# A decoder layer on one core: the last output projection of the second stage issued at twice the density, with new orders on four engines behind it

## The chip, the core and the metric

The kernel runs on one NeuronCore of a Trainium2 chip. The metric is the time of one execution on the device, in microseconds, taken as the median of several runs. The engines that matter here are TensorE (PE in the rows, with PEld for its weight loads), VectorE (DVE), ScalarE (ACT), GpSimd (POOL) and SyncE (SP), which only issues DMAs. Each engine works through its own queue strictly in the order in which the program wrote it; engines wait for one another by semaphores.

## The reference

The input is 32 sequences ("tiles", 0 to 31) of 128 rows by 1024 columns, and a context of the same size. For each tile:

```python
x = _layernorm(x + _L0_attn_ref(x, wq, wk, wv, wo))      # causal attention, 32 heads, 8 kv heads
x = _layernorm(x + _L0_xattn_ref(x, ctx, weight))        # 3-tap convolution, inputs scaled by cosine similarities
x = _layernorm(x + _L0_ffn_ref(x, A, B, Wr, br))         # 8 rank-16 adapters weighted by a softmax router
# in _L0_xattn_ref:
out = jnp.einsum('bit,oi->bot', inp_unf * att, w_flat)   # inp_unf: 3 shifted copies, att: similarities, repeated
# in _L0_ffn_ref:
low = jnp.einsum('bsd,hrd->bshr', x, A)                  # rank reduction, 1024 -> 128 (and 8 router logits)
out = jnp.einsum('bshr,hor,bsh->bso', low, B, scores)    # gates, then expansion 128 -> 1024
```

Everything is float32. Large products are made of three TensorE passes: both operands are split into a high part and the rest (`hi`, `lo`), and high x high, high x rest and rest x high are added in PSUM.

## The kernel before

The program has two stages in one launch. The first makes the attention of every tile and stores it. The second, `part2`, takes each tile through the output projection, the first norm, the convolution, the second norm, the adapters and the third norm. The change lies in the end of the second stage alone.

**The second stage is a software pipeline over tiles.** In step t the engines work on four tiles at once, by the names in the code `o = t` (projection), `c = t-1` (first norm and convolution), `f = t-2` (second norm, rank reduction, router) and `z = t-3` (expansion, third norm). `steps` runs `step(t, ...)` for the last tiles unrolled; what is left of the last tiles after step 31 is written out by hand behind it. Which instruction comes next on an engine is decided by that text and by nothing else.

What each function issues:

- PE: `project(t, par, n, k)` issues 3 passes, 48 in all for a tile, 24 into each half `wo_ps0`, `wo_ps1`. `convolve(t, m)`, m = 0 to 5, issues 3 passes and needs product m; m = 0 to 2 is the first half of the columns, 3 to 5 the second. `turn_x2` makes 4 transposes of the second norm's result, `reduce_rank` contracts these to 136 columns (`low_done`), `turn_low` transposes the gated result, `expand` issues 6 passes.
- DVE: `add(t, par, n, half)` adds the residual to the result of stage n (0 projection, 1 convolution, 2 adapters), `count` takes its statistics and `average` mean and variance. `multiply(t, par, m)` makes product m (similarities times shifted rows). `route`, `gate_low` and `low_lt` serve the adapters.
- ACT: `normalise1`, `normalise2`, `normalise3` apply the three norms, `high_prod(t, m)` makes the high part of product m, `copy_x2` fetches the transposes from PSUM, `gates` the exponentials, `high_lt` the high part of the turned gated result.
- POOL: `invert_root(t, n)` makes the scale of norm n and its shift (the pair at lines 1482 and 1484), `low_prod(t, m)` the rest of product m. One product therefore passes DVE, ACT, POOL and PE, in this order, and three buffers (`PB = 3`) are in flight.

**The last step before.** In step 31 PE has 16 slots, one projection triple in each, and between them, by the table `CONV_AT`, what belongs to tiles 28, 29 and 30: convolutions of tile 29 (products 4, 5), of tile 30 (0 to 3), the expansion of tile 28, the transposes and rank reduction of tile 29. Then, by hand, come products 4 and 5 of tile 30, the expansion of tile 29, the convolution of tile 31 with the transposes of tile 30 behind its second product, and the adapters of tiles 30 and 31. The accumulators of the adapters of tile 30 are `wo_ps`, since the projection no longer needs them; the others use `ffn_ps`. Line numbers of the profile in this part: L1134 projection, L1145 convolution, L1160 transposes, L1167 rank reduction, L1173 `turn_low`, L1179 expansion, L1237, L1242 and L1247 the three additions, L1254 statistics, L1271 products, L1382 high parts, L1387, L1393 and L1416 the three norms, L1399 `copy_x2`, L1405 gates, L1410 `high_lt`, L1488 the rest of a product.

Of the kernel before, what the change touches and what calls it, by code (L numbers as in the profile page):

```python
# [22 lines left out]
B, S, D = 32, 128, 1024  # L23
P = 128
KT = D // P
# [33 lines left out]
def after(t, per, k):  # L59

    return t * per + k
# [917 lines left out]
def part2(nc, ctx, weights, raw, halves, wo_ps, handoff, x, wa, br, ident, ot_dram, sim_dram, out):  # L979
# [12 lines left out]
    PB = 3  # L992
# [64 lines left out]
    LEAD, TAIL = 6, 5  # L1057
    UNITS = 2 * TAPS
# [67 lines left out]
    def _(pe):  # L1126
# [36 lines left out]
        def reduce_rank(t):  # L1163

            wait(pe, xt_in, after(t, 2, 2))
            for k in range(KT):
                mm = pe.matmul(ffn_place(t)[0][:, 0:LOWW], xt[:, k], wa_t[:, k * LOWW:(k + 1) * LOWW],  # L1167
                               start=(k == 0), stop=(k == KT - 1))
            mm.then_inc(low_done, 1)

        def turn_low(t):
            wait(pe, gated_done, after(t, 1, 1))
            pe.transpose(ffn_place(t)[1][:, 0:S], gated[:], id_t[:]).then_inc(low_turned, 1)  # L1173
# [26 lines left out]
                if valid(o) and not at_step(o, 0) and not (at_step(o, 1) and s < KT):  # L1200
                    project(o, par, s // KT, s % KT)

        steps(pe, step, 0, B - 1, LEAD, TAIL - 3)

        convolve(B - 2, 4)
        turn_low(B - 3)
        convolve(B - 2, 5)
        expand(B - 3)
        for m in range(UNITS):
            convolve(B - 1, m)  # L1210
            if m == 1:
                turn_x2(B - 2, 0, 0)
                turn_x2(B - 2, 0, 1)
        reduce_rank(B - 2)
        turn_x2(B - 1, 1, 0)
        turn_low(B - 2)
        turn_x2(B - 1, 1, 1)
        expand(B - 2)
        reduce_rank(B - 1)
# [4 lines left out]
    def _(dve):  # L1224
# [25 lines left out]
        def count(t, n, half):  # L1250

            src = y3 if n == 2 else yz[n]
            dve.wait_ge(added[n], after(t, 2, half + 1))
            dve.bn_stats(stats[n][:, half], src[:, half * BANK:(half + 1) * BANK]).then_inc(counted[n], 1)  # L1254
# [79 lines left out]
            if valid(f):  # L1334
                gate_low(f)

        steps(dve, step, 0, B - 1, LEAD, TAIL - 3)

        def finish(t):

            for half in range(2):
                add(t, t % 2, 2, half)
                count(t, 2, half)
            average(t, 2)

        add(B - 1, 1, 0, 1)
        count(B - 1, 0, 1)
        average(B - 1, 0)
        low_lt(B - 3)
        add(B - 2, 0, 1, 1)  # L1350
        count(B - 2, 1, 1)
        average(B - 2, 1)
        for m in range(PB):
            multiply(B - 1, 1, m)
        finish(B - 3)
        for m in range(PB, UNITS):
            multiply(B - 1, 1, m)
        add(B - 1, 1, 1, 0)
        count(B - 1, 1, 0)
        add(B - 1, 1, 1, 1)  # L1360
        count(B - 1, 1, 1)
        average(B - 1, 1)
        route(B - 2)
        gate_low(B - 2)
        low_lt(B - 2)
        finish(B - 2)
# [6 lines left out]
    def _(act):  # L1373
# [73 lines left out]
            if valid(c):  # L1447
                high_prod(c, 5)

        steps(act, step, 0, B - 1, LEAD, TAIL - 3)  # L1450

        high_lt(B - 3)
        normalise1(B - 1, 1)
        normalise2(B - 2, 0)
        for m in range(UNITS):
            high_prod(B - 1, m)
            if m in (2, 3):
                copy_x2(B - 2, m - 2)
        normalise3(B - 3, 1)
        normalise2(B - 1, 1)  # L1460
        gates(B - 2)
        copy_x2(B - 1, 0)
        high_lt(B - 2)
        copy_x2(B - 1, 1)
        gates(B - 1)
        high_lt(B - 1)
# [3 lines left out]
    @block.gpsimd  # L1470
    def _(pool):
        def low_o(t, par, half):
            cols = slice(half * D // 2, (half + 1) * D // 2)
            wait(pool, o_hi, after(t, 1, 1))
            hi, lo = (os_t[:, par, part].rearrange("p t s -> p (t s)")[:, cols] for part in range(2))
            pool.tensor_tensor(lo, oraw[:, par, cols], hi.bitcast(F32), ALU.subtract).then_inc(o_lo, 1)  # L1476

        def invert_root(t, n):

            wait(pool, var_done[n], after(t, 1, 1))  # L1480
            wait(pool, normed[n], after(t - 1, 1, 1))
            pool.tensor_tensor(rstd[n][:], var[n][:], power[:], ALU.pow).then_inc(rstd_done[n], 1)  # L1482
            pool.wait_ge(rstd_done[n], after(t, 1, 1))
            pool.tensor_tensor(shift[n][:], nmean[n][:], rstd[n][:], ALU.mult).then_inc(shifted[n], 1)

        def low_prod(t, m):
            wait(pool, prod_hi, after(t, UNITS, m + 1))
            pool.tensor_tensor(prods[:, m % PB, 1], prod[:, m % PB], prods[:, m % PB, 0].bitcast(F32),  # L1488
                               ALU.subtract).then_inc(prod_lo, 1)

        pool.wait_ge(set_up, 3)

        def step(t, par):
            c, f, z = t - 1, t - 2, t - 3
            early = not at_step(t, 0) and not at_step(t, 1)
            if valid(c):
                invert_root(c, 0)
            if at_step(t, 1):
                low_o(2, 0, 0)
                low_o(2, 0, 1)  # L1500
            if valid(t + 1) and early:
                low_o(t + 1, 1 - par, 0)
            if valid(c):
                low_prod(c, 0)
            if valid(f):
                invert_root(f, 1)
            if valid(c):
                low_prod(c, 1)
            if valid(z):
                invert_root(z, 2)  # L1510
            if valid(c):
                low_prod(c, 2)
            if valid(t + 1) and early:
                low_o(t + 1, 1 - par, 1)
            if valid(c):
                for m in range(3, UNITS):
                    low_prod(c, m)

        steps(pool, step, 0, B - 1, LEAD, TAIL - 3)

        invert_root(B - 1, 0)
        invert_root(B - 2, 1)
        for m in range(UNITS):
            low_prod(B - 1, m)
            if m == 2:
                invert_root(B - 3, 2)
        invert_root(B - 1, 1)
        invert_root(B - 2, 2)
        invert_root(B - 1, 2)
# [48 lines left out]
```

## Time and profile before

| | us |
|---|---|
| median of three runs | 1408.07 |
| lowest and highest of them | 1407.62, 1410.24 |
| span of the profiled execution, first to last instruction | 1404.9 |
| what the median has beyond that span (1408.07 - 1404.9) | 3.2 |
| busy in the span: PE, DVE, POOL, ACT | 1359.3, 1094.9, 984.3, 931.8 |
| last projection triple of tile 31 ends, in the span | 1363.7 |
| last norm of tile 31 ends (1400.54 + 1.24) | 1401.8 |

Of the profiled execution only the span is given; what lies around its first and last instruction is taken as the 3.2 us of the table. A step of the second stage lasts 19.5 us (in the chain of waits the first four transposes of a tile come at 1336.51 and of the next at 1356.03). The clock that is granted to TensorE is 1.00 of full speed in nearly all of the span; its dips lie in the last 40 us.

### The profile page before, as it was taken

Reading aid. Unit: us, or ns where it says so; the run is one execution under the profiler, and the core shown is the slowest. Engines: PE = TensorE matmul, PEld = TensorE weight load, DVE = VectorE, ACT = ScalarE, POOL = GpSimd, SP = SyncE. Lnnn points to the kernel's source line nnn. Section 1 sums busy time; section 2 is a strip of 40 time slices with the busy share of each in tenths; the row PEclk is TensorE's granted clock in tenths of the full one; section 3 lists DMA queues with packets and bytes.
Section 4 is the critical chain, followed back from the end, with each engine's and each line's share of the span. In section 5 each row is a group of like instructions: output and inputs, shape, how many; then the busy total and the mean of one; then the engine's idle time right before and its main releaser. Section 6 shows DMA issues by size and latency. Waiting matters only on the chain.

```text
span 1404.9 us, 32306 instructions
## 1 busy us (share of the span) xinstructions
PE 1359.3 (97%) x8294; PEld 1058.0 (75%) x8294; DVE 1094.9 (78%) x3869; ACT 931.8 (66%) x3258; POOL 984.3 (70%) x936
## 2 busy tenths in 40 slices
PE   8999999999999999999986999999999999999995
PEld 6777777777777777777754788888888888888873
DVE  5887887878788787787775678887788877888774
ACT  5888888878788887888884455554555545555443
POOL 4777776777777677777774667766777667776653
PEclk9999999999999999999998999999999999999997
DMA  7354545445453544545478865657656666676751
GB/s 264 96 152 123 159 116 158 128 136 159 114 159 117 155 137 129 159 115 164 124 208 242 181 162 157 166 153 171 157 157 165 156 171 156 160 161 158 157 120 45
DMA packets 108861, 213.03 MB, mean 152 GB/s; under 512 B 26640, under 2 KB 32272, under 8 KB 108816
## 3 DMA queue, kind: packets, MB, share of 16 engines
q1 hardware_dynamic: 108480, 211.73, 56.5%
q10 hardware_dynamic: 336, 0.79, 0.2%
q8 instruction: 18, 0.29, 0.1%
q14 instruction: 27, 0.22, 0.1%
HBM read 131.83 MB, written 34.47 MB: 118 GB/s over the span
## 4 chain that ended last, share of the span: by engine, by line
PE 87%; POOL 3%; DMA 2%; SPq 2%; DVE 2%; issue 2%; ACT 2%; ACTq 0%; DVEq 0%; POOLq 0%
PE wo_ps L479 34%; PE wo_ps L1134 23%; PE conv_ps L1145 9%; PE s_ps L509 5%; PE pv_ps L522 4%; PE ffn_ps L1167 4%; PE ffn_ps L1179 3%; PE ffn_ps L1160 2%; PE turn_ps L498 2%; SPq L320 1%; POOL prods L1488 1%; ACT pexp L767 1%; DMA pt<-in_wqkv 1%; DMA raw<-in_xT 1%; PE turn_ps L488 0%
## 5 line engine op out<-in xcount | busy, mean ns | idle before, releaser
L479 PE MATMUL wo_ps<-weights,halves 128*128 128x512 f32 x2304 | 570.7, 400 | 3.5 <-DVE weights L681 3.5
L479 PEld LDWEIGHTS wo_ps<-weights,halves 128*128 128x128 f32 x2304 | 422.8, 189 | 137.8 <-issue 53.8
L767 ACT ACTIVATE pexp<-sm,smin 128x128 f32<-128x128 f32 x1024 | 398.0, 391 | 99.0 <-DVE smin L618 98.0
L1134 PE MATMUL wo_ps<-weights,halves 128*128 128x512 f32 x1464 | 393.2, 401 | 1.0 <-PEq L143 1.0
L1488 POOL TENSOR_TENSOR prods<-prod,prods 128x512 fp32r<-128x512 f32 x192 | 259.3, 1359 | 131.0 <-ACT prods L1382 126.0
L906 POOL TENSOR_TENSOR pn<-pexp,prec 128x512 f32<-128x512 f32 x256 | 265.4, 1041 | 98.1 <-DVE prec L625 98.1
L1134 PEld LDWEIGHTS wo_ps<-weights,halves 128*128 128x128 f32 x1464 | 267.1, 189 | 58.1 <-issue 1.8
L618 DVE CUSTOM_DVE_ANT_0 sm<-s_ps,mask_t 128x128 f32<-128x128 f32 x1024 | 231.9, 282 | 24.9 <-PE s_ps L509 19.6
L1382 ACT CAST prods<-prod 128x512 fp32r<-128x512 f32 x192 | 118.9, 621 | 165.5 <-DVE prod L1271 127.9
L1271 DVE TENSOR_TENSOR prod<-att,x 128x512 f32<-128x512 f32 x192 | 186.6, 987 | 13.3 <-DMA att<-sim_scratch 8.4
L767 ACT ACTIVATION_READ_ACCUMULATOR pexp<-sm,smin 128x1 f32 x1024 | 193.4, 189 | 0.0
L633 DVE STREAM_TRANSPOSE blocks<-pn 128x512 f32<-128x512 f32 x256 | 178.0, 695 | 6.6 <-POOL pn L906 6.3
L1145 PE MATMUL conv_ps<-prods,weights 128*128 128x512 f32 x576 | 169.4, 403 | 12.6 <-POOL prods L1488 12.6
L1145 PEld LDWEIGHTS conv_ps<-prods,weights 128*128 128x128 f32 x576 | 109.1, 191 | 40.9 <-POOL prods L1488 16.7
L901 POOL TENSOR_TENSOR xn<-rot,y 128x512 f32<-128x512 f32 x64 | 83.7, 1308 | 70.9 <-DVE y L605 70.8
L1254 DVE BATCH_NORM_STATS2 stats<-y 128x6 f32<-128x512 f32 x190 | 128.8, 691 | 4.5
L1482 POOL TENSOR_TENSOR moments<-moments,power 128x1 f32<-128x1 f32 x96 | 76.6, 798 | 64.2 <-DVE moments L1262 62.8
L880 POOL TENSOR_TENSOR halves<-raw,halves 128x512 fp32r<-128x512 f32 x62 | 80.7, 1302 | 27.1 <-ACT halves L740 27.1
L625 DVE RECIPROCAL prec<-psum_row 128x4 f32<-128x4 f32 x256 | 44.9, 175 | 69.8 <-ACT pexp L767 69.8
L600 DVE TENSOR_TENSOR rot<-wo_ps,rope_t 128x512 f32<-128x512 f32 (+1 forms) x96 | 56.7, 591 | 45.9 <-PE wo_ps L479 44.1
L1476 POOL TENSOR_TENSOR halves<-raw,halves 128x512 fp32r<-128x512 f32 x60 | 90.8, 1515 | 0.0
L618 DVE DVE_READ_ACCUMULATOR2_ANT smin<- 128x1 f32 x1024 | 85.0, 83 | 0.0
(103 smaller groups left out, 1636.5 us busy)
## 6 DMA issues: line engine op xcount, KB each, us to landing
att<-sim_scratch SPq DMA_DIRECT2D x192, 252.0 KB
pt<-blocks SPq DMA_DIRECT2D x636, 64.0 KB, 2.0
ctx_t<-in_ctx SPq DMA_DIRECT2D x32, 576.0 KB, 5.2
raw<-in_xT SPq DMA_DIRECT2D x32, 512.0 KB, 3.9
xn<-in_x SPq DMA_DIRECT2D x32, 512.0 KB, 7.6
out<-late SPq DMA_DIRECT2D x32, 512.0 KB, 6.2
ot_scratch<-ot SPq DMA_DIRECT2D x63, 256.0 KB, 2.1
raw<-ot_scratch SPq DMA_DIRECT2D x31, 512.0 KB, 6.8
```

Of the source, the lines that this page charges most:

```text
L479: mm = pe.matmul(qkv_ps[(par + g) % 2][:], xs[:, par, xl, k], w_sb[:, wl, g, k], start=(k == 0 and n == 0), stop=(k == KT - 1 and n == 2))
L618: ins = dve.tensor_tensor_reduce(sm[:, c % 2, i * P:(i + 1) * P], s_ps[i][:, j * P:(j + 1) * P], mask_t[:], 1.0, 3e38, ALU.add, ALU.min, s ...
L633: dve.transpose(blocks[:, u, :, j], pn[:, c % 2].rearrange("p (i b k) -> p b i k", i=NI, b=QB)).then_inc(turned, 1)
L767: ins = nc.scalar.activation(pexp[:, c % 2, i * P:(i + 1) * P], sm[:, c % 2, i * P:(i + 1) * P], ACT.Exp, bias=smin[:, c % 2, i:i + 1], sc ...
L906: pool.tensor_tensor(pn[:, c % 2].rearrange("p (i s) -> p i s", i=NI), pexp[:, c % 2].rearrange("p (i s) -> p i s", i=NI), prec[:, c % 2]. ...
L1134: mm = pe.matmul(wo_ps[n][:], os_t[:, par, ol, k], wo_sb[:, wl, k, n * BANK:(n + 1) * BANK], start=(k == 0 and m == 0), stop=(k == KT - 1 ...
L1145: mm = pe.matmul(conv_ps[h][:], wx_sb[:, wl, k], prods[:, m % PB, xl], start=(k == 0 and n == 0), stop=(k == TAPS - 1 and n == 2))
L1254: dve.bn_stats(stats[n][:, half], src[:, half * BANK:(half + 1) * BANK]).then_inc(counted[n], 1)
L1271: dve.tensor_tensor(prod[:, m % PB], att[:, k, h * BANK:(h + 1) * BANK], x1[:, par, h * BANK + k:h * BANK + k + BANK], ALU.mult).then_inc( ...
L1382: nc.scalar.copy(prods[:, m % PB, 0], prod[:, m % PB]).then_inc(prod_hi, 1)
L1476: pool.tensor_tensor(lo, oraw[:, par, cols], hi.bitcast(F32), ALU.subtract).then_inc(o_lo, 1)
L1488: pool.tensor_tensor(prods[:, m % PB, 1], prod[:, m % PB], prods[:, m % PB, 0].bitcast(F32), ALU.subtract).then_inc(prod_lo, 1)
```

## The change

The loop of steps now ends with step 30, and step 31 is written out by hand. On PE it has eight slots with two projection triples each, so that the 48 passes of tile 31 come with less of other work between them: the transposes, rank reduction and expansion of tile 29 and products 3 to 5 of tile 30 are moved behind the projection. In the convolution of tile 31 the transposes of tile 30 stand ahead of product 4, no longer ahead of product 2, and its rank reduction ahead of product 5. DVE, ACT and POOL get new orders to go with it. No arithmetic is added or taken away.

```diff
-        steps(pe, step, 0, B - 1, LEAD, TAIL - 3)
+        steps(pe, step, 0, B - 2, LEAD, TAIL - 4)
+        for s in range(KT):
+            if s == 1:
+                convolve(B - 3, 4)
+                turn_low(B - 4)
+            if s == 3:
+                expand(B - 4)
+            if s == 4:
+                convolve(B - 3, 5)
+            if s > 4:
+                convolve(B - 2, s - 5)
+            for k in (2 * s, 2 * s + 1):
+                project(B - 1, 1, k // KT, k % KT)
+        turn_x2(B - 3, 1, 0)
+        turn_x2(B - 3, 1, 1)
+        convolve(B - 2, 3)
+        reduce_rank(B - 3)
         convolve(B - 2, 4)
+        convolve(B - 2, 5)
         turn_low(B - 3)
-        convolve(B - 2, 5)
         expand(B - 3)
         for m in range(UNITS):
-            convolve(B - 1, m)
-            if m == 1:
+            if m == 4:
                 turn_x2(B - 2, 0, 0)
                 turn_x2(B - 2, 0, 1)
-        reduce_rank(B - 2)
+            if m == 5:
+                reduce_rank(B - 2)
+            convolve(B - 1, m)
+        turn_low(B - 2)
         turn_x2(B - 1, 1, 0)
-        turn_low(B - 2)
         turn_x2(B - 1, 1, 1)
...
# DVE, of the order written out for step 31 and behind it
+        add_and_count(B - 1, 0, 1)
         average(B - 1, 0)
+        multiply(B - 2, 0, 5)
+        add_and_count(B - 2, 1, 0)
+        route(B - 3)
+        multiply(B - 1, 1, 0)
+        gate_low(B - 3)
+        multiply(B - 1, 1, 1)
         low_lt(B - 3)
+        multiply(B - 1, 1, 2)
+        add_and_count(B - 2, 1, 1)
         average(B - 2, 1)
+        add(B - 3, 1, 2, 0)
+        add(B - 3, 1, 2, 1)
+        multiply(B - 1, 1, 3)
...
# ACT
+        high_prod(B - 1, 1)
+        high_prod(B - 1, 2)
         normalise2(B - 2, 0)
+        high_prod(B - 1, 3)
+        copy_x2(B - 2, 0)
+        high_prod(B - 1, 4)
+        copy_x2(B - 2, 1)
+        high_prod(B - 1, 5)
...
# POOL
+        low_prod(B - 1, 0)
+        low_prod(B - 1, 1)
         invert_root(B - 2, 1)
-        for m in range(UNITS):
+        for m in range(2, UNITS):
             low_prod(B - 1, m)
-            if m == 2:
-                invert_root(B - 3, 2)
+        invert_root(B - 3, 2)
```

PE at the start of step 31. In the kernel before, from the last triple of tile 30 and the first of tile 31 on:

```order
 L1134 MATMUL wo_ps<-weights,halves 128x512 x3
-L1134 MATMUL wo_ps<-weights,halves 128x512 x6
-L1145 MATMUL conv_ps<-prods,weights 128x512 x3
-L1173 MATMUL ffn_ps<-id_t,gated 128x128
-L1134 MATMUL wo_ps<-weights,halves 128x512 x6
-L1179 MATMUL ffn_ps<-weights,lt 128x512 x6
-L1134 MATMUL wo_ps<-weights,halves 128x512 x3
-L1145 MATMUL conv_ps<-prods,weights 128x512 x3
-L1134 MATMUL wo_ps<-weights,halves 128x512 x15
+L1134 MATMUL wo_ps<-weights,halves 128x512 x9
+L1145 MATMUL conv_ps<-prods,weights 128x512 x3
+L1173 MATMUL ffn_ps<-id_t,gated 128x128
+L1134 MATMUL wo_ps<-weights,halves 128x512 x12
+L1179 MATMUL ffn_ps<-weights,lt 128x512 x6
+L1134 MATMUL wo_ps<-weights,halves 128x512 x6
+L1145 MATMUL conv_ps<-prods,weights 128x512 x3
```

Ahead of the expansion of tile 28 (L1179) stood three triples of tile 31 (the first x6 row holds one of tile 30), and now six; ahead of the convolution that ends tile 29 (the second L1145) stood four, and now eight.

PE in the convolution of tile 31, before (the accumulators' numbers are shown; `wo_ps` holds the transposes and the rank reduction of tile 30):

```order
L1145 MATMUL conv_ps0<-prods,weights 128x512 x6
L1160 MATMUL wo_ps0<-id2_t,late 128x128 x4
L1160 MATMUL wo_ps1<-id2_t,late 128x128 x4
L1145 MATMUL conv_ps0<-prods,weights 128x512 x3
L1145 MATMUL conv_ps1<-prods,weights 128x512 x9
L1167 MATMUL wo_ps0<-wa_t,xt 128x136 x8
```

And now:

```order
L1145 MATMUL conv_ps0<-prods,weights 128x512 x9
L1145 MATMUL conv_ps1<-prods,weights 128x512 x3
L1160 MATMUL wo_ps0<-id2_t,late 128x128 x4
L1160 MATMUL wo_ps1<-id2_t,late 128x128 x4
L1145 MATMUL conv_ps1<-prods,weights 128x512 x3
L1167 MATMUL wo_ps0<-wa_t,xt 128x136 x8
L1145 MATMUL conv_ps1<-prods,weights 128x512 x3
```

The transposes have moved from behind the second product to behind the fourth, and the rank reduction from behind the last product to ahead of it.

DVE from the first norm of tile 31 to product 3 of tile 31, before:

```order
L1262 TENSOR_SCALAR moments<-mv0 128x1
L1294 TENSOR_TENSOR lt<-ffn_ps1,lt 128x128
L1242 TENSOR_TENSOR y1<-conv_ps1,x1 128x512
L1254 BN_STATS stats1<-y1 128x6
L1259 BN_AGGR mv1<-stats1 128x2
L1261 TENSOR_SCALAR moments<-mv1 128x1
L1262 TENSOR_SCALAR moments<-mv1 128x1
L1271 TENSOR_TENSOR prod<-att,x1 128x512 x3
```

And now (line numbers are those of the changed text, L1288 a product, L1259 the addition of the convolution):

```order
L1288 TENSOR_TENSOR prod<-att,x1 128x512
L1302 RECIPROCAL grec<-gsum 128x1
L1304 SCALAR_TENSOR_TENSOR gated<-ffn_ps0,grec,gate 128x128
L1288 TENSOR_TENSOR prod<-att,x1 128x512
L1311 TENSOR_TENSOR lt<-ffn_ps1,lt 128x128
L1288 TENSOR_TENSOR prod<-att,x1 128x512
L1259 TENSOR_TENSOR y1<-conv_ps1,x1 128x512
L1271 BN_STATS stats1<-y1 128x6
L1276 BN_AGGR mv1<-stats1 128x2
L1278 TENSOR_SCALAR moments<-mv1 128x1
```

The second half of tile 30's convolution is now added behind the first three products of tile 31, where it was added ahead of them, and between those products stand the gating and `low_lt` of tile 29.

## Rows read from the trace of the kernel before

**Rows 1.** Stretches: length; busy (instructions) of each engine; PEclk; DMA share; GB/s.
```profile
1320.00:1340.00 20.00, 20.00 (x100) 16.61 (x99) 16.24 (x34) 10.30 (x16) 14.62 (x15) 1.00 0.65 137
...
1372.00:1376.80 4.80, 4.80 (x15) 3.95 (x16) 3.87 (x7) 1.03 (x3) 3.52 (x4) 0.50 0.02 5
1376.80:1383.50 6.70, 5.32 (x28) 3.67 (x26) 2.94 (x5) 2.74 (x5) 3.76 (x3) 1.00 0.20 78
1383.50:1387.00 3.50, 0.87 (x6) 0.55 (x6) 1.00 (x7) 1.81 (x4) 0.74 (x2) 1.00 0.00 0
1387.00:1390.40 3.40, 3.40 (x11) 2.69 (x12) 1.08 (x3) 1.09 (x3) 0.00 (x0) 0.51 0.00 0
```

**Rows 2.** Timeline of PE: start, length, instruction, count, [idle before <-released by].
```profile
1346.86 1.56 PE L1179 MATMUL ffn_ps<-weights,lt 128*128 128x512 f32 x6
...
1348.95 0.86 PE L1145 MATMUL conv_ps<-prods,weights 128*128 128x512 f32 x3
1349.65 3.60 PE L1134 MATMUL wo_ps<-weights,halves 128*128 128x512 f32 x15
...
1362.79 0.86 PE L1134 MATMUL wo_ps<-weights,halves 128*128 128x512 f32 x3
...
1371.95 2.93 PE L1145 MATMUL conv_ps<-prods,weights 128*128 128x512 f32 x6 [4.32 <-POOL prods L1488]
1374.68 1.91 PE L1160 MATMUL wo_ps<-id_t,late 128*128 128x128 f32 x8
...
1378.29 0.96 PE L1145 MATMUL conv_ps<-prods,weights 128*128 128x512 f32 x3 [0.82 <-POOL prods L1488]
...
1380.77 0.96 PE L1145 MATMUL conv_ps<-prods,weights 128*128 128x512 f32 x3 [0.27 <-POOL prods L1488]
1381.57 2.01 PE L1167 MATMUL wo_ps<-wa_t,xt 128*128 128x136 f32 x16
1386.01 0.66 PE L1160 MATMUL ffn_ps<-id_t,late 128*128 128x128 f32 x4 [2.43 <-ACT late L1393]
...
1387.89 2.84 PE L1179 MATMUL wo_ps<-weights,lt 128*128 128x512 f32 x6
```

**Rows 3.** Timeline of DVE.
```profile
1349.86 0.69 DVE L1242 TENSOR_TENSOR y<-conv_ps,x 128x512 f32<-128x512 f32 x1
...
1363.69 0.69 DVE L1237 TENSOR_TENSOR y<-wo_ps,xn 128x512 f32<-128x512 f32 x1 [0.66 <-PE wo_ps L1134]
...
1368.03 1.89 DVE L1271 TENSOR_TENSOR prod<-att,x 128x512 f32<-128x512 f32 x3 [0.18 <-ACT x L1387]
...
1373.26 2.88 DVE L1271 TENSOR_TENSOR prod<-att,x 128x512 f32<-128x512 f32 x3
...
1381.77 0.69 DVE L1242 TENSOR_TENSOR y<-conv_ps,x 128x512 f32<-128x512 f32 x1 [2.85 <-PE conv_ps L1145]
...
1389.58 0.69 DVE L1247 SCALAR_TENSOR_TENSOR y<-wo_ps,late 128x512 f32<-128x512 f32 x1 [1.74 <-PE wo_ps L1179]
```

**Rows 4.** Timeline of POOL.
```profile
1351.95 0.93 POOL L1482 TENSOR_TENSOR moments<-moments,power 128x1 f32<-128x1 f32 x1 [0.17 <-DVE moments L1262]
...
1353.20 1.30 POOL L1488 TENSOR_TENSOR prods<-prod,prods 128x512 fp32r<-128x512 f32 x1
...
1370.63 3.74 POOL L1488 TENSOR_TENSOR prods<-prod,prods 128x512 fp32r<-128x512 f32 x3 [1.86 <-ACT prods L1382]
```

**Rows 5.** Timeline of ACT.
```profile
1366.65 1.24 ACT L1387 ACTIVATE x<-y,moments 128x1024 f32<-128x1024 f32 x1 [1.89 <-POOL moments L1484]
...
1375.77 0.59 ACT L1399 COPY xt<-wo_ps 128x512 f32<-128x512 f32 x1 [4.18 <-PE wo_ps L1160]
1376.26 0.62 ACT L1382 CAST prods<-prod 128x512 fp32r<-128x512 f32 x1
...
1384.72 1.24 ACT L1393 ACTIVATE late<-y,moments 128x1024 f32<-128x1024 f32 x1 [5.18 <-POOL moments L1484]
...
1400.54 1.24 ACT L1416 ACTIVATE late<-y,moments 128x1024 f32<-128x1024 f32 x1 [4.51 <-POOL moments L1484]
```

More of the change, by code:

```diff
@@ L1335, in step, with add_and_count @@
                 gate_low(f)
-        steps(dve, step, 0, B - 1, LEAD, TAIL - 3)
+        steps(dve, step, 0, B - 2, LEAD, TAIL - 4)
+        def add_and_count(t, n, half):
+            add(t, t % 2, n, half)
+            count(t, n, half)
         def finish(t):
             for half in range(2):
-                add(t, t % 2, 2, half)
-                count(t, 2, half)
+                add_and_count(t, 2, half)
             average(t, 2)
-        add(B - 1, 1, 0, 1)
-        count(B - 1, 0, 1)
-        average(B - 1, 0)
+        add_and_count(B - 2, 0, 1)
+        average(B - 2, 0)
+        low_lt(B - 4)
+        add(B - 4, 0, 2, 0)
+        add(B - 4, 0, 2, 1)
+        multiply(B - 2, 0, 0)
+        add_and_count(B - 3, 1, 1)
+        average(B - 3, 1)
+        multiply(B - 2, 0, 1)
+        count(B - 4, 2, 0)
+        count(B - 4, 2, 1)
+        average(B - 4, 2)
+        multiply(B - 2, 0, 2)
+        add_and_count(B - 1, 0, 0)
+        multiply(B - 2, 0, 3)
+        multiply(B - 2, 0, 4)
+        add_and_count(B - 1, 0, 1)
+        average(B - 1, 0)
+        multiply(B - 2, 0, 5)
[4 more added lines that the diff above has]
+        multiply(B - 1, 1, 1)
         low_lt(B - 3)
-        add(B - 2, 0, 1, 1)
-        count(B - 2, 1, 1)
+        multiply(B - 1, 1, 2)
+        add_and_count(B - 2, 1, 1)
         average(B - 2, 1)
[L1353 to L1361, printed above, removed]
+        add(B - 3, 1, 2, 0)
+        add(B - 3, 1, 2, 1)
+        multiply(B - 1, 1, 3)
+        count(B - 3, 2, 0)
+        multiply(B - 1, 1, 4)
+        count(B - 3, 2, 1)
+        average(B - 3, 2)
+        multiply(B - 1, 1, 5)
+        add_and_count(B - 1, 1, 0)
+        route(B - 2)
+        add_and_count(B - 1, 1, 1)
         average(B - 1, 1)
-        route(B - 2)
         gate_low(B - 2)
@@ L1448, in step @@
                 high_prod(c, 5)
-        steps(act, step, 0, B - 1, LEAD, TAIL - 3)
+        steps(act, step, 0, B - 2, LEAD, TAIL - 4)
+        high_lt(B - 4)
+        normalise1(B - 2, 0)
+        high_prod(B - 2, 0)
+        high_prod(B - 2, 1)
+        normalise2(B - 3, 1)
+        high_prod(B - 2, 2)
+        normalise3(B - 4, 0)
+        high_prod(B - 2, 3)
+        high_prod(B - 2, 4)
+        copy_x2(B - 3, 0)
+        copy_x2(B - 3, 1)
+        high_prod(B - 2, 5)
+        normalise1(B - 1, 1)
+        gates(B - 3)
+        high_prod(B - 1, 0)
         high_lt(B - 3)
-        normalise1(B - 1, 1)
+        high_prod(B - 1, 1)
+        high_prod(B - 1, 2)
         normalise2(B - 2, 0)
-        for m in range(UNITS):
-            high_prod(B - 1, m)
-            if m in (2, 3):
-                copy_x2(B - 2, m - 2)
+        high_prod(B - 1, 3)
[3 more added lines that the diff above has]
+        high_prod(B - 1, 5)
         normalise3(B - 3, 1)
+        gates(B - 2)
         normalise2(B - 1, 1)
-        gates(B - 2)
+        high_lt(B - 2)
         copy_x2(B - 1, 0)
-        high_lt(B - 2)
         copy_x2(B - 1, 1)
@@ L1517, in step @@
                     low_prod(c, m)
-        steps(pool, step, 0, B - 1, LEAD, TAIL - 3)
+        steps(pool, step, 0, B - 2, LEAD, TAIL - 4)
+        invert_root(B - 2, 0)
+        low_prod(B - 2, 0)
+        invert_root(B - 3, 1)
+        low_prod(B - 2, 1)
+        invert_root(B - 4, 2)
+        for m in range(2, 5):
+            low_prod(B - 2, m)
         invert_root(B - 1, 0)
+        low_prod(B - 2, 5)
+        low_prod(B - 1, 0)
+        low_prod(B - 1, 1)
         invert_root(B - 2, 1)
-        for m in range(UNITS):
+        for m in range(2, UNITS):
             low_prod(B - 1, m)
-            if m == 2:
-                invert_root(B - 3, 2)
+        invert_root(B - 3, 2)
         invert_root(B - 1, 1)
```

## Prediction

> **What bounds the kernel now.** I read the stretches first. In the middle of the second stage TensorE is busy for all of the 20 us from 1320 to 1340, at full clock, and every other engine has room [rows 1]. Up to the last projection, then, only what PE has to do decides. Behind it the picture turns: the timeline of PE shows idle 4.32, 0.82 and 0.27 us for `low_prod`, then 2.43 us for the second norm [rows 2], and the chain goes from one engine to the next. So a change that only shuffles PE's work can gain up to the last projection, by putting it first, and from there on the orders of DVE, ACT and POOL count as much. I then followed the last 60 us engine by engine [rows 2 to 5], and worked the new order with the same durations and the same gaps between engines. All times below are in the scale of the old trace, "was" is its value.
>
> **The clock.** PEclk was 0.50 from 1372 to 1376.8, after the idle 4.32 us, and 0.51 from 1387 to 1390.4, after 2.43 us [rows 1, 2]: that is 1.2 in place of 2.4 GHz. The trace gives prices: two convolutions 2.93 us, eight transposes 1.91, an expansion 2.84, against 0.86 for one convolution, 0.66 for four transposes and 1.56 for an expansion at full clock [rows 2].
>
> **Step 1, the head of step 31.** 15 passes take 3.60 us with 0.16 of emptying at the end, so a triple has 0.69 [rows 2]; I use 0.70, for a convolution too, 0.11 for `turn_low` and 1.40 for an expansion. Step 31 starts three triples, a convolution and `turn_low` ahead of 1346.86, at 1343.96. Now six triples stand ahead of the expansion of tile 28: it comes at 1348.97, 2.1 late. Eight stand ahead of the convolution that ends tile 29: 1343.96 + 9 x 0.70 + 0.11 + 1.40 = 1351.8, was 1348.95, 2.8 late. DVE adds it at 1352.7, was 1349.86 [rows 3]; behind that addition, in the unchanged order of DVE, wait the norm of tile 29 and products 1 to 4 of tile 30, all 2.8 late. What hid the old wait of these products was slack against PE's position; that cover is now gone.
>
> **Step 2, the projection.** Without waits it would end after 16 triples, 5 convolutions, `turn_low` and an expansion, 1343.96 + 21 x 0.70 + 1.51 + 0.16 = 1360.3; was 1362.79 + 0.86 = 1363.65 [rows 2]: 3.3 earlier. But POOL makes the root of tile 29 at 1351.95 and the rest of product 1 at 1353.20 for 1.30 [rows 4], now 2.8 later: ready at 1357.3. PE stands ready for it at 1351.8 + 6 x 0.70 = 1356.0 and waits 1.3. Product 2 is ready about 2.6 after product 1 (its low part of 1.30 and the root of another norm at some 1.25 lie behind the low part of product 1, as that lies 1.25 behind the root at 1351.95): PE, ready at 1359.4, waits 0.5. The projection ends at 1362.2, a lead of 1.5, and not of 3.3. The two loads of similarities for tile 31 are issued 2.8 later as well, their cover is the time to product 0 of tile 31 (some 9 us); they cost nothing.
>
> **Step 3, the first norm of tile 31.** DVE adds at 1362.2 (was 1363.69). Between the mean and the norm there now stands product 5 of tile 30 on DVE (0.68) and its high part on ACT (0.62), ahead of `normalise1` in ACT's queue: 1362.2 + 1.95 (addition and statistics at 0.69 each, the mean, and what lies between them) + 0.68 + 0.04 + 0.62 = 1365.5. `normalise1` was at 1366.65 [rows 5]: a lead of 1.1.
>
> **Step 4, where the lead goes.** Before, DVE added the second half of tile 30 while it waited for this norm. Now it does so behind three products of tile 31, `gate_low` and `low_lt`. Three products in a row took 1.89 us, but 2.88 where POOL was making low parts at the same time (1373.26, POOL at work from 1370.63 to 1374.37) [rows 3, 4]; an operation held like that ends about 0.55 after POOL's. So product 0 starts at 1366.9, product 2 at 1368.9 and ends, held by POOL, at 1370.2. The addition ends at 1370.8, statistics and mean take 1.4 more, and POOL needs 0.9 for root and shift [rows 4]; the low part of product 2 stands behind them, 1373.1 to 1374.4. Its old place was the last third of 1370.63 to 1374.37 [rows 4]. The lead is nil. Product 3, held until 1374.9, is where it was.
>
> **Step 5, the last three products.** High part 1375.0 to 1375.6, low part (0.35 held) to 1377.3, convolution 3 at 1377.35, was 1378.29 [rows 2]: there ACT stood at `copy_x2` until 1375.77, waiting for the transposes, with the high part of product 3 behind it [rows 5]. Now both come later. Transposes at full clock to 1378.65, `copy_x2` 1378.7, only then the high part of product 4, 1379.2 to 1379.8, its low part to 1381.1, and convolution 4 at 1381.2. Product 5 is ready at 1382.4, but ahead of it stands the rank reduction, from 1381.9, which holds PE 1.85 (16 passes of 0.115; 2.01 with emptying [rows 2]): convolution 5 at 1383.7. It was at 1380.77. **DVE adds it at 1384.6, was 1381.77 [rows 3]: 2.85 late.** In the old order the transposes lay in time in which PE waited for POOL, and the rank reduction behind the last convolution, beside the addition and the mean. This is the term on which the forecast stands.
>
> **Step 6, the tail.** `normalise2` of tile 31 comes at 1384.72 + 2.85 = 1387.6 [rows 5], and ends at 1388.8. Now the gating of tile 30 is done ahead of it, so the expansion can follow the transposes directly: 1389.7, first half at DVE 1390.6, at full clock. It was at 1389.58 [rows 3], with the expansion at half clock. From that addition on nothing changes, and it was 12.2 to the end of the last norm at 1401.78 [rows 3, 5]. Sum at full clock throughout: +1.05.
>
> Now the clock. By the steps above PE is idle about 2.3 us before convolution 2 of tile 31 (from 1372.1), 2.2 before convolution 3, 2.2 before convolution 4 and 2.6 behind convolution 5, with only 0.86 of work between the first two. The stretch with 0.87 us of work in 3.50 was followed by half clock [rows 1]. So I count half clock twice: at convolution 3 and the transposes of tile 30 (2.93 / 2 - 0.86 = 0.6, and 1.91 / 2 - 0.66, 0.3 to 0.4, on the chain), 1.0; and at the transposes of tile 31 and the first half of the expansion of tile 30 (1.91 - 1.3 = 0.6 and 2.84 / 2 - 0.78 = 0.65, with the first pass after idle longer), 1.3 to 1.6. Together 1.05 + 1.0 + 1.5 = **+3.55**. The span becomes 1404.9 + 3.55 = 1408.45; with the 3.17 that the median has beyond the span, and so 1408.07 + 3.55 = **1411.6**. The order's own cost in this is bounded from below by the +1.05 and from above by a rank reduction at half clock, for which no row exists: between nothing and a doubling, 1.85 more. I take nothing, since the reduction follows 2 to 3 us of work, as the one at 1381.57 did; the range keeps it.
>
> The Trainium skill, "TensorE: Matmul & The Clock Gate", section "Why this matters for your kernels", asks for no idle gap of more than about 3 us between bursts of matmuls, or the clock drops. By it none of the new gaps would cost anything, and the sum would be +1.05. The trace disagrees: 2.43 us of idle time, with little work before, were followed by 0.51 [rows 1, 2]. I give it the second rival.
>
> **Rivals.** (A change below 0.2%, 2.8 us, can't be told from none in a measurement of this kernel.)
>
> *Faster.* The lead of 1.1 at the first norm of tile 31 lives on to the last convolution. For it: PE was idle 4.32 us there, and now has tile 29 to do in it, so that the clock may stay at 1.00, which was worth 0.6 on each convolution. It decides at POOL: if the low part of product 2 comes at 1371.5 and not behind the root of tile 30, product 3 follows at once, and the last convolution ends at 1380.6. With the tail at full clock (-1.4): 1408.07 - 1.1 - 1.4 = 1405.5. Against it: the order on POOL is strict, and the rank reduction still stands ahead of the last convolution.
>
> *The clock stays at full.* +1.05 alone: 1409.1. For it: gaps of 2.2 to 2.6 us are much shorter than 4.32. Against it: 2.43 was enough once.
>
> *Rank reduction at half clock as well,* and with it a third piece of the tail: 3.55 + 1.85 = +5.4, 1413.5.
>
> *The projection doesn't come earlier.* If DVE's products are held longer than in the old rows, PE waits for each of products 0 to 2 of tile 30 and the last triple ends where it did. Everything behind follows 1.1 later at most, since `normalise1` then has no lead: 1412.7. For it: POOL and DVE meet more often in the new order; against it: the five waits of step 2 are known from rows, and 1.8 us of the 3.3 are already counted as lost.
>
> **How the numbers follow.** The forecast, with half clock once or twice, +2.3 to +4.6: 0.52. Full clock: 0.18. Rank reduction at half clock: 0.11. No earlier projection: 0.09. Faster: 0.10. Slower than 1410.9 (1408.07 + 2.8) are nine tenths of the forecast's share less the cases at one dip, 0.43, and the two late cases, 0.20: 0.63. Faster than 1405.3: a little less than the faster case, 0.07, as its 1405.5 lies on the bound. The rest, 0.30, is no difference. The range reaches from 1407.5, which takes in full clock and leaves out the faster case, to 1414.5, beyond the case of 1413.5.
>
> **What would show it.** Right: last projection triple ends near 1362; `normalise1` of tile 31 near 1365.5; the low part of product 2 of tile 31 still at 1373, behind a root; PE idle before convolutions 2, 3 and 4 of tile 31 about 2 us each; the last convolution at 1383 to 1385, directly behind the rank reduction; PEclk 0.5 in a part of 1376 to 1391. Wrong: the last addition of the convolution before 1382, or a rank reduction that ends before its product is ready.

## The result, and the profile after

| | before | changed |
|---|---|---|
| median, us | 1409.57 | 1413.80 |
| lowest and highest | 1407.62, 1410.24 | 1409.80, 1414.49 |
| ratio, with its 95% interval | | 1.0029 [1.0018, 1.0041] |
| span of the profiled execution | 1404.9 | 1412.0 |
| start of step 31 to the end of the last norm | 57.8 | 62.8 |

The changed kernel is slower by 0.29% +- 0.11, some 4.1 us; 3.55 were forecast (the medians are over six runs each, three of them the ones shown before). The spans differ by 7.1, but 2.15 of this lie ahead of the change: the first triple of tile 31 starts at 1346.12 in the one execution and at 1343.97 in the other, though the program is the same up to there (over the profiles of this study that start lies between 1343.97 and 1347.83). So the two tails are compared from that triple on. For this result and the ten runs below, the timed difference to the kernel before and the difference of the tails differ by 1.4 us at most, by 0.1 on the mean: nothing points to a loss ahead of the tail. In the last line of the table and below, "at 18.2" is 18.2 us behind it.

PE after, from the last triple of tile 30 on (timeline: start, length, instruction, count, idle before it and its releaser); the rows answer to those of PE before [rows 2]:

```profile
1345.42 2.24 PE L1134 MATMUL wo_ps<-weights,halves 128*128 128x512 f32 x9
...
1353.82 0.87 PE L1145 MATMUL conv_ps<-prods,weights 128*128 128x512 f32 x3
...
1359.40 0.96 PE L1145 MATMUL conv_ps<-prods,weights 128*128 128x512 f32 x3 [1.01 <-POOL prods L1547]
1360.20 1.56 PE L1134 MATMUL wo_ps<-weights,halves 128*128 128x512 f32 x6
1361.97 0.97 PE L1145 MATMUL conv_ps<-prods,weights 128*128 128x512 f32 x3 [0.22 <-POOL prods L1547]
1362.78 1.55 PE L1134 MATMUL wo_ps<-weights,halves 128*128 128x512 f32 x6
...
1376.63 0.97 PE L1145 MATMUL conv_ps<-prods,weights 128*128 128x512 f32 x3 [1.93 <-POOL prods L1547]
1379.50 1.65 PE L1145 MATMUL conv_ps<-prods,weights 128*128 128x512 f32 x3 [1.90 <-POOL prods L1547]
1380.95 1.91 PE L1160 MATMUL wo_ps<-id_t,late 128*128 128x128 f32 x8
1384.54 1.65 PE L1145 MATMUL conv_ps<-prods,weights 128*128 128x512 f32 x3 [1.68 <-POOL prods L1547]
1385.98 3.04 PE L1167 MATMUL wo_ps<-wa_t,xt 128*128 128x136 f32 x16
1388.77 0.95 PE L1145 MATMUL conv_ps<-prods,weights 128*128 128x512 f32 x3
```

The x9 row holds one triple of tile 30, so step 31 starts at 1345.42 + 0.70. The reader is to see three things. The convolution that ends tile 29 comes at 1353.82, 7.7 behind the start, where it came at 5.0. PE waits 1.01 and 0.22 us for products of tile 30, and the last triple ends at 1364.33, at 18.2, where it ended at 19.7. And of the last three convolutions each has its own obstacle: the wait for product 3, then the transposes and a new wait, then the whole rank reduction, which runs ahead of the last one. That last one ends at 43.6; it ended at 37.8.

DVE, ACT and POOL after, the rows that answer to [rows 3 to 5]:

```profile
1372.45 0.68 DVE L1259 TENSOR_TENSOR y<-conv_ps,x 128x512 f32<-128x512 f32 x1
...
1375.57 1.56 DVE L1288 TENSOR_TENSOR prod<-att,x 128x512 f32<-128x512 f32 x1
...
1389.76 0.69 DVE L1259 TENSOR_TENSOR y<-conv_ps,x 128x512 f32<-128x512 f32 x1 [0.34 <-PE conv_ps L1145]
```

```profile
1374.54 0.55 POOL L1541 TENSOR_TENSOR moments<-moments,power 128x1 f32<-128x1 f32 x1 [0.85 <-DVE moments L1279]
1375.16 0.19 POOL L1543 TENSOR_TENSOR moments<-moments 128x1 f32<-128x1 f32 x1
1375.31 1.27 POOL L1547 TENSOR_TENSOR prods<-prod,prods 128x512 fp32r<-128x512 f32 x1
```

```profile
1367.71 1.24 ACT L1429 ACTIVATE x<-y,moments 128x1024 f32<-128x1024 f32 x1
...
1382.04 0.58 ACT L1441 COPY xt<-wo_ps 128x512 f32<-128x512 f32 x1 [4.26 <-PE wo_ps L1160]
1382.52 0.62 ACT L1424 CAST prods<-prod 128x512 fp32r<-128x512 f32 x1
...
1392.71 1.24 ACT L1435 ACTIVATE late<-y,moments 128x1024 f32<-128x1024 f32 x1 [2.86 <-POOL moments L1543]
```

The first norm of tile 31 starts at 21.6 (22.7 before), but POOL makes the low part of its product 2 only behind the root of tile 30, at 29.2 (29.1 before). The high part of product 4 stands behind `copy_x2`, which waits 4.26 us for the transposes. The second norm of tile 31 starts at 46.6; it started at 40.8.

The clock after (stretches: length; busy and instructions of PE, PEld, DVE, ACT, POOL; PEclk; DMA; GB/s), to be set beside [rows 1]:

```profile
1378.00:1388.00 10.00, 6.82 (x23) 5.73 (x24) 3.24 (x8) 3.35 (x5) 4.64 (x5) 0.50 0.00 1
1388.00:1394.80 6.80, 2.86 (x19) 2.19 (x19) 2.85 (x10) 1.89 (x5) 0.74 (x2) 0.99 0.19 77
1394.80:1398.30 3.50, 3.50 (x13) 2.92 (x12) 1.78 (x3) 0.98 (x2) 0.00 (x0) 0.51 0.00 0
```

Ten microseconds in a row at half clock, over the transposes and most of the rank reduction that now stand on the chain, and over two convolutions.

### The profile page after: what moved, and what is told of

Its sections match the earlier page's. It is cut to its first block, busy times and chain, and to the rows that moved or that the text cites. A ratio compares the mean times of both kernels' runs of the same rounds, so it can differ in the third digit from the quotient of the medians.

```text
span 1412.0 us, 32306 instructions
## 1 busy us (share of the span) xinstructions
PE 1362.4 (96%) x8294; PEld 1058.7 (75%) x8294; DVE 1094.0 (77%) x3869; ACT 932.3 (66%) x3258; POOL 984.2 (70%) x936
## 4 chain that ended last, share of the span: by engine, by line
PE 80%; DMA 5%; SPq 5%; DVE 3%; issue 3%; POOL 2%; ACT 2%; ACTq 0%; DVEq 0%; POOLq 0%
PE wo_ps L479 29%; PE wo_ps L1134 23%; PE conv_ps L1145 9%; PE s_ps L509 4%; PE ffn_ps L1167 4%; PE pv_ps L522 4%; SPq L320 3%; PE ffn_ps L1179 3%; DMA raw<-in_xT 2%; PE ffn_ps L1160 2%; PE turn_ps L498 1%; DMA att<-sim_scratch 1%; ACT pexp L767 1%; DMA pt<-in_wqkv 1%; DVE sm L618 1%
## 5 line engine op out<-in xcount | busy, mean ns | idle before, releaser
L1288 DVE TENSOR_TENSOR prod<-att,x 128x512 f32<-128x512 f32 x192 | 187.4, 990 | 14.0 <-DMA att<-sim_scratch 11.2
L1145 PE MATMUL conv_ps<-prods,weights 128*128 128x512 f32 x576 | 169.3, 402 | 12.8 <-POOL prods L1547 12.7
L1145 PEld LDWEIGHTS conv_ps<-prods,weights 128*128 128x128 f32 x576 | 108.2, 190 | 41.9 <-POOL prods L1547 17.9
L625 DVE RECIPROCAL prec<-psum_row 128x4 f32<-128x4 f32 x256 | 44.9, 175 | 75.8 <-ACT pexp L767 75.8
L509 PEld LDWEIGHTS s_ps<-kt,qt 32*128 32x128 f32 x2048 | 64.0, 188 | 29.2 <-issue 23.9
```

Of the source, the lines that this page charges most:

```text
L509: mm = pe.matmul(s_ps[i][:, j * P:(j + 1) * P], qt[rows, u, j * P:(j + 1) * P], kt[rows, par, u * P:(u + 1) * P], start=True, stop=True, t ...
L1288: dve.tensor_tensor(prod[:, m % PB], att[:, k, h * BANK:(h + 1) * BANK], x1[:, par, h * BANK + k:h * BANK + k + BANK], ALU.mult).then_inc( ...
```

## The experiments

All ratios are to the kernel before, run beside them on the same chip. The tail is the time from the first triple of tile 31 to the end of the last norm in the one profiled execution; it was 57.8 before and 62.8 changed. A second profile of the changed kernel, `changed_again` below, has 61.7; the kernel before has only one.

**The last two products: the rank reduction alone.**

```diff
-            if m == 5:
-                reduce_rank(B - 2)
             convolve(B - 1, m)
+        reduce_rank(B - 2)
```

with `route(B - 2)` behind `average(B - 1, 1)` on DVE.

> The changed kernel with the rank reduction of tile 30 behind the last convolution of tile 31, not ahead of it, and its router behind the mean of tile 31 on DVE. If the order of PE at the last two products is what costs (my theory), the last convolution no longer waits for 16 passes: about 2.1 us less than the changed kernel, so 1.0014 of the kernel before. If the time is lost in the head of step 31 and in the second norm of tile 30 (the first rival), the last product is late anyway and nothing moves: 1.0029. If only TensorE's clock costs (the second rival), nothing moves either, or up to 1 us for the reduction that the changed kernel ran at half clock.

Measured 1.0025 [1.0015, 1.0036], tail 61.0. The last convolution started at 39.6, not at 42.7, and the second norm of tile 31 at 44.8, not at 46.6. But the reduction moved to where it ran at half clock:

```profile
1386.23 0.97 PE L1145 MATMUL conv_ps<-prods,weights 128*128 128x512 f32 x3 [1.68 <-POOL prods L1546]
1387.47 1.21 PE L1145 MATMUL conv_ps<-prods,weights 128*128 128x512 f32 x3 [0.27 <-POOL prods L1546]
1388.47 3.46 PE L1167 MATMUL wo_ps<-wa_t,xt 128*128 128x136 f32 x16
```

A miss in time: the 1.0014 expected lies just outside, and the gain on the changed kernel is 0.0004, with about 0.0010 to either side of both ratios. Against `changed_again`, where the reduction ran at full clock, the last convolution starts 1.4 earlier (39.6, 41.0), so the reduction did stand in its way, but the second norm of tile 31 comes no earlier (44.8, 44.9). The rows of POOL and ACT say why:

```profile
1391.44 0.20 POOL L1542 TENSOR_TENSOR moments<-moments 128x1 f32<-128x1 f32 x1
```

```profile
1392.37 0.30 ACT L1446 ACTIVATE gate<-logit,nmax 128x8 f32<-128x8 f32 x1 [2.90 <-DVE nmax L1297]
...
1392.67 1.22 ACT L1434 ACTIVATE late<-y,moments 128x1024 f32<-128x1024 f32 x1
```

The scale of the norm is ready at 1391.64, but `gates` of tile 30 stands ahead of the norm in ACT's queue (in the kernel before it stood behind it), and waits for the late and slow reduction: 1.0 us. The edit took the reduction off PE's way to the last convolution and left it on the chain through ACT.

**The last two products: the transposes alone.**

```diff
-            if m == 4:
+            if m == 3:
                 turn_x2(B - 2, 0, 0)
                 turn_x2(B - 2, 0, 1)
```

> The changed kernel with the transposes of tile 30 one product earlier, ahead of the convolution of product 3 and not of product 4; nothing else. My theory: PE waits 1.9 us for product 3 there, the second norm of tile 30 is ready, so the transposes cost nothing, ACT gets its copies before the high part of product 4 and is no longer held: about 3.7 us less than the changed kernel, 1.0003 of the kernel before. First rival (head and second norm): no change, 1.0029. Clock rival: a little less, since PE's idle time is cut in two: 1.0022.

Measured 0.9998 [0.9989, 1.0007], tail 58.9. In the timed runs this one number moved takes back the loss, as expected, and both rivals as priced (1.0029 and 1.0022) fall; in the profiles the tail is 3.9 shorter than in the first execution of the changed kernel and 2.8 shorter than in the second, and still 1.1 longer than before. The rows of PE:

```profile
1374.50 1.28 PE L1145 MATMUL conv_ps<-prods,weights 128*128 128x512 f32 x3 [1.93 <-POOL prods L1547]
1375.58 1.91 PE L1160 MATMUL wo_ps<-id_t,late 128*128 128x128 f32 x8
1377.37 1.40 PE L1145 MATMUL conv_ps<-prods,weights 128*128 128x512 f32 x3
1379.55 0.96 PE L1145 MATMUL conv_ps<-prods,weights 128*128 128x512 f32 x3 [0.78 <-POOL prods L1547]
1380.35 2.02 PE L1167 MATMUL wo_ps<-wa_t,xt 128*128 128x136 f32 x16
1382.12 0.95 PE L1145 MATMUL conv_ps<-prods,weights 128*128 128x512 f32 x3
```

Product 3's convolution is no later (33.4 in both), product 4's comes at 35.6 and not at 38.4, and the wait ahead of it is 0.78 and not 1.68. The last convolution starts at 38.1. In `changed_again` it starts at 41.0, with the transposes at half clock and the rank reduction at full clock as here, so these 2.8 us are the order's above all.

**The clock.** Extra passes into an unused bank, where PE waits, in the changed kernel and in the one before:

```diff
+                pe.matmul(spare[:], wx_sb[:, 0, 0], wb_sb[:, 0, 0:BANK], start=True, stop=True)
...
+            fill((0, 0, 6, 6, 5, 0)[m])
             convolve(B - 1, m)
+        fill(8)
         turn_low(B - 2)
...
```

> The changed kernel with extra passes on PE into an unused PSUM bank where it waits in the tail: 6, 6 and 5 of 512 columns ahead of the convolutions of products 2, 3 and 4 of tile 31, 8 ahead of turn_low of tile 30, 4 each ahead of the transposes of tile 31 and turn_low of tile 31. They keep the clock at full speed and should end before what PE waits for. My sum at full clock: the order alone costs 1.05 us against the kernel before as it is, so 1.0007. If the clock costs nothing on the chain: 1.0029. If the clock is all of the loss: 1.0000 or below.

> The kernel before with such passes where PE waits: 14 ahead of the convolution of product 0 of tile 31, 8 ahead of the transposes of tile 31, 4 ahead of its turn_low. If the half clock from 1372 to 1376.8 and from 1387 to 1390.4 lies on the chain as I took it, about 1.9 us go: 0.9987 of the kernel before. If half clock only makes PE's waits shorter: 1.0000.

Measured 1.0019 [1.0009, 1.0029], tail 59.2, and 0.9993 [0.9985, 1.0002], tail 56.7. The timed runs leave this open: the first interval leaves out 1.0007 by little and reaches to 1.0029, the second holds 0.9987 and 1.0000 alike. The traces say more. In the changed kernel the clock is then full through the stretches in which it had dipped:

```profile
1377.00:1388.00 11.00, 9.52 (x53) 7.56 (x51) 5.48 (x13) 4.05 (x8) 4.81 (x5) 1.00 0.09 35
1388.00:1399.00 11.00, 7.88 (x45) 5.97 (x44) 5.27 (x18) 4.21 (x8) 1.48 (x4) 1.00 0.03 13
```

Its tail is 1.4 us longer than that of the kernel before, where the sum at full clock had 1.05; its last convolution started at 39.9, where the sum had 39.7. So half clock cost the changed kernel up to 3.6 us in the first profiled execution and up to 2.5 in `changed_again`. The ratios of the timed runs say less, 0.0010, some 1.4 us, with intervals that overlap. In the kernel before 1.1 us went of the 1.9 expected; the last expansion still ran at half clock for a part in it (6 passes in 2.77 us, against 1.67), as it did in the filled changed kernel (2.21). Between the two filled kernels, each with such a rest of half clock, the order costs 2.5 us in the traces.

**The head and the tail, each undone.** First, the expansion of tile 28 and the last convolution of tile 29 back at their places of before in step 31:

```diff
...
+                if k == 3:
+                    expand(B - 4)
+                if k == 4:
+                    convolve(B - 3, 5)
                 project(B - 1, 1, k // KT, k % KT)
```

> The changed kernel with the expansion of tile 28 behind three triples of tile 31 and the convolution of product 5 of tile 29 behind four, as in the kernel before; all else as changed. My theory of the head (steps 1 and 2 of the prediction): DVE gets the second norm of tile 29 about 2.8 us earlier, PE waits less for products 1 and 2 of tile 30, the projection ends 1.8 us earlier than in the changed kernel, at 16.4 us behind the start of step 31 and not 18.2; some of it is lost again at the late transposes, 1.4 us at the end of the kernel: 1.0019 of the kernel before. Rival: the lead is lost again in the second norm of tile 30, as the first 1.1 us were: 1.0029.

Measured 1.0012 [1.0001, 1.0023], tail 59.3. The projection ended at 16.4 and the first norm of tile 31 started at 19.8, 1.8 earlier than in the changed kernel, and PE waited for products 1 and 2 of tile 30 no longer. The last convolution started at 39.2, again 1.8 earlier than in `changed_again` (41.0), in both with the rank reduction at full clock: the head's delay is real and reaches the last product, so the rival falls by the rows. The timed gain of 0.0017 has intervals that overlap.

Then the order of before from the first norm of tile 31 on (`average(B - 2, 1)`, `normalise2(B - 2, 0)` and `invert_root(B - 2, 1)` ahead of the products of tile 31, transposes behind product 1, rank reduction last):

> The changed kernel up to the first norm of tile 31 on all engines, and from there the order of the kernel before: second norm of tile 30 ahead of the products of tile 31 on DVE, ACT and POOL, transposes behind product 1, rank reduction behind product 5. If the new order of the last three products is what costs, and the head is a gain: 1.0 to 1.5 us less than the changed kernel, but not all of it, since the second norm of tile 30 now stands between the first norm of tile 31 and its products: 1.0018. If the tail's new order were a gain in itself: above 1.0029.

Measured 1.0015 [1.0005, 1.0025], tail 59.0. As expected: the products of tile 31 start later (its first convolution at 30.0, not at 26.7), and the last starts at some 38.1 all the same, against 42.7 and 41.0.

**Both small repairs.** The edits of `early_turns` and `old_head` together.

> The changed kernel with both small repairs: expansion of tile 28 and convolution of product 5 of tile 29 at their old places in the head, transposes of tile 30 ahead of product 3 and not of product 4. If the two losses are apart from each other, their gains add: early_turns measured 0.9998, and the head gave 0.0017 more: 0.998. If both gains are the same microseconds: 0.9998.

Measured 0.9989 [0.9979, 1.0000], tail 57.4. The interval holds both expected numbers, so the timed runs don't say whether the gains add; the tail is 1.5 shorter than in `early_turns`, though the rank reduction ran at half clock in this execution (3.2 us).

**The changed kernel once more.**

> The changed kernel once more, beside the two repaired ones on the same chip: 1.0029 again. Its tail in the trace, from the first projection triple of tile 31 to the end of the last norm, was 62.8 us against 57.8, of which I put down 3.6 to half clock, as the version with added passes has 59.2; with less half clock this execution should lie between 59.2 and 62.8.

Measured 1.0037 [1.0024, 1.0050], tail 61.7, between the two as expected. At product 4 it stands where the first execution did, to 0.02 us (38.40 and 38.42). Then its rank reduction ran in 2.02 us, at full clock, and the last convolution started at 41.0, where the first execution had 42.7:

```profile
1374.92 1.65 PE L1145 MATMUL conv_ps<-prods,weights 128*128 128x512 f32 x3 [1.93 <-POOL prods L1547]
...
1379.24 1.91 PE L1160 MATMUL wo_ps<-id_t,late 128*128 128x128 f32 x8
1382.83 0.96 PE L1145 MATMUL conv_ps<-prods,weights 128*128 128x512 f32 x3 [1.68 <-POOL prods L1547]
1383.63 2.02 PE L1167 MATMUL wo_ps<-wa_t,xt 128*128 128x136 f32 x16
1385.40 0.96 PE L1145 MATMUL conv_ps<-prods,weights 128*128 128x512 f32 x3
```

The clock fell earlier than in the first execution, and was back for the reduction (stretches as above):

```profile
1373.00:1374.74 1.74, 0.00 (x0) 0.00 (x0) 1.74 (x3) 1.05 (x1) 1.66 (x3) 1.00 0.00 0
1374.74:1381.57 6.83, 5.00 (x14) 3.39 (x14) 4.80 (x10) 2.04 (x5) 1.78 (x3) 0.50 0.00 1
```

**A better order.** If the gaps between the engines are known, the order can be chosen by them. This version has the same instructions in other orders on all four engines from step 31 on.

> A version of my own: the same instructions, in orders for all four engines from step 31 on that were worked out from the durations of the old trace. Expansion of tile 28 and convolution of tile 29 early, projection ended at 15.5 us behind the start of step 31, second norm of tile 30 between products 1 and 2 of tile 31, transposes of tile 30 ahead of product 2, the finish of tile 29 behind all products of tile 31. If the chain is as I have it, POOL makes the last four low parts back to back and the last convolution starts 4 us earlier than in the kernel before: 7 us less at the end, 0.995 of the kernel before. If the second half is bound by something else (clock, the port that DVE and POOL share), half of that: 0.9975.

Measured 1.0012 [0.9999, 1.0025], tail 59.1: a miss. The projection ended at 14.7 and the first norm of tile 31 started at 18.3. Then this, on DVE and in the queue of SyncE:

```profile
1369.22 0.70 DVE L1301 TENSOR_TENSOR prod<-att,x 128x512 f32<-128x512 f32 x1
1378.46 1.89 DVE L1301 TENSOR_TENSOR prod<-att,x 128x512 f32<-128x512 f32 x3 [8.54 <-DMA att<-sim_scratch]
```

```profile
1369.75 0.38 SPq L1117 DMA_DIRECT2D out<-late  x1
1370.18 1.70 SPq L1087 DMA_DIRECT2D att<-sim_scratch  x3
1371.93 0.65 SPq L1092 DMA_DIRECT2D att<-sim_scratch  x1
```

The load of the second half of tile 31's similarities stands behind the store of tile 28, and that waits for the third norm of tile 28, which this order has late (ACT, at 1368.48). The order had been worked out over four engines; the fifth queue held it. PE shows the price of a rank reduction wholly at half clock (0.50 from 1380.8 to 1384.5), behind a wait of 7.26 us:

```profile
1380.83 3.99 PE L1167 MATMUL wo_ps<-wa_t,xt 128*128 128x136 f32 x16 [7.26 <-ACT xt L1460]
```

One more edit, on SyncE, puts the load ahead of the store:

```diff
+            if at_step(t, B - 1):
+                load_att(t, 1)
             if valid(t - 3):
                 wait(sp, normed[2], after(t - 3, 1, 1))
                 sp.dma_start(out[t - 3], res[:, 1 - par]).then_inc(stored[1 - par], 16)
...
```

> The reordered version with one more edit: on SyncE the load of the second half of tile 31's similarities is issued ahead of the store of tile 28, not behind it. In the reordered version product 3 of tile 31 waited 8.5 us for that load, because the store ahead of it in SyncE's queue waits for the third norm of tile 28, which that order has late. If this queue was what took the gain: the last convolution starts 4 us earlier than in the kernel before, 0.995 of its time. If the load is late by itself (its transfer takes longer than I think), or another wait takes the place: 0.998 or above.

Measured **0.9953 [0.9939, 0.9967]**, 1402.16 us against 1409.37, tail 51.3. The last of the three convolutions in the first row below starts at 32.6, 4.2 earlier than in the kernel before (36.8). The store of tile 28 now stands behind the load:

```profile
1375.29 2.34 PE L1147 MATMUL conv_ps<-prods,weights 128*128 128x512 f32 x9
```

```profile
1360.19 1.21 SPq L1087 DMA_DIRECT2D att<-sim_scratch  x3
1361.45 0.64 SPq L1092 DMA_DIRECT2D att<-sim_scratch  x1
1368.29 27.55 SPq L1119 DMA_DIRECT2D out<-late  x4
```

## Why the prediction was right, point by point

**Steps 1 to 4 (head, projection, first norm, lost lead) held.** Forecast, behind the start of step 31, and measured: end of the projection 18.2, 18.2; first norm of tile 31 21.5, 21.6; low part of product 2 29.1, 29.2. The waits for products 1 and 2 of tile 30 were forecast at 1.3 and 0.5 and show as 1.01 and 0.22; 0.16 of each difference is the emptying, behind which the profile begins to count. `old_head` shows that the delay of step 1 is what took the other 1.8 us of the lead.

**Step 5 (the last three products) held, and `early_turns` shows that it decides.** Convolution 3 was forecast at 33.4 and came at 33.4. The last one was forecast at 39.7 at full clock, and one dip added 1.0: 40.7, against 41.0 in `changed_again`. In the first profiled execution it was 42.7, later than the 39 to 41 (1383 to 1385) that the prediction gave as its sign. What the step left out there is the rank reduction at half clock: I took nothing for it, as it follows 2 to 3 us of work. But transposes and a convolution of work had not brought the clock back, and the reduction took 3.04 us for 2.01, with product 4's convolution at 1.65 for 0.96. The doubling that I gave as its upper bound, 1.85 more, is reached in `reordered`, where all 16 passes took 3.99 (3.46 in `late_rank`, at half clock for most of them).

**Step 6 (tail) held, with a clock term that fits one execution of two.** From the start of the second norm of tile 31 to the end of the last norm the sum had 15.3 at full clock and 16.8 with a dip; the profiles show 16.2 (`after`), 16.8 (`changed_again`), and 15.3 in `after_filled`. So the dip of 1.5 was 0.9 in the first execution: the eight transposes took 1.16 there, and 1.97 in the second.

**The clock as a term** was counted at 2.5 us for two dips. The traces have 3.6 and 2.5 (`after`, `changed_again`, less `after_filled`); the timed runs have 1.4 with an interval of some 2 to either side. Its size is not settled to better than that, and as the kernel before was profiled once, how much its own dips vary is not shown. The timed loss of 4.1 has an interval from 2.5 to 5.8 us, and the two profiles have 5.0 and 3.9, so that the forecast of 3.55 comes so near is in part luck; the reduction at half clock, which the sum put at nothing, is the main difference between the two (1.7 at the last convolution). Where the dips fall differs from one execution to the next, and with it up to 1.1 us of the tail of one and the same program.

**The 3.17 us beyond the span** are not what lies around an execution: every profiled run that has both numbers shows 2.1 (1414.09 and 1412.0). The forecast doesn't hang on it, since the 3.55 was added to the median.

**The rivals.** "The clock stays at full": it did not, though PE was never idle for more than 2.6 us in the tail. What was said for it, that the new gaps are much shorter than 4.32, left out when the clock had fallen in the kernel before: at 1370.0, 2.4 us into that wait.

```profile
1370.02:1376.80 6.78, 4.85 (x15) 4.00 (x16) 5.78 (x10) 2.60 (x7) 4.89 (x5) 0.50 0.01 4
```

By the rule on idle gaps in the Trainium skill ("TensorE: Matmul & The Clock Gate", section "Why this matters for your kernels") nothing would have been lost; the traces disagree. In the first execution the clock fell at 1377.8, 0.2 us into a wait, with 0.97 of work and a wait of 1.93 before it, and stayed at 0.50 for ten microseconds. In `changed_again` it fell 1.74 us into a single wait. "Rank reduction at half clock" took place in one of two profiled executions, whose tail of +5.0 is nearer to this rival's +5.4 than to the forecast. "No earlier projection": it ended 1.5 earlier. "Faster": the lead was at nil where step 4 put it, behind the root of tile 30 on POOL.

## What to carry to other kernels

Where a chain goes through four in-order engines, a step that is put first pays only if what it displaces was not feeding the next item; list for each displaced instruction who stands behind it in the queue. Side work belongs where its engine waits and its input is already there, and ahead of the step that needs its result: ahead of product 3 eight transposes held up nothing, ahead of product 4 they put the last convolution 2.8 us later. What is moved off one engine's chain can still hold another's queue, as `gates` did in `late_rank`. And an order that is worked out from durations must include the DMA-issuing queue: one store ahead of one load turned 0.9953 into 1.0012.

## What the runs showed of the hardware that I had not expected

TensorE fell to half clock and stayed there for 10.2 us (1377.83 to 1388.07) though no idle time was above 1.93 us and it was busy for 6.82 of 10.00 us by the profile. In another execution of the same program the clock fell at 1374.74, 1.74 us into a wait, and was back at 1381.57. Sixteen rank-reduction passes of 136 columns take 2.02 us at full clock and 3.99 at half, so even such small passes pay in full. And the time up to step 31, in which all these programs are the same, varied by 3.9 us between profiled executions, about as much as the change itself.
